# A new order for the attention tile of a decoder kernel, with row-tiled scores and column-tiled value weighting

## What is computed

```python
def _layer(x, wqkv, qs, ksc, wo, lg, lb, w1, b1, w2, b2):   # twice, 8 heads of 64
    qkv = shift_token(x) @ wqkv
    ...
    q, k = l2norm(q) * qs, l2norm(k) * ksc
    q, k = rotary_xpos(q, k)
    # window w of 128 tokens sees the keys of windows w-1 and w, causal and masked
    sim = einsum('bhwid,bhwjd->bhwij', q * 8, look_around(k))
    o = einsum('bhwij,bhwjd->bhwid', softmax(where(mask, -max, sim)), look_around(v))
    x = x + o @ wo
    ...                                      # then layer norm, gated gelu MLP, residual
```

## Time and profile before

| | us |
|---|---|
| median of 3 runs | 1198.59 (1198.31 to 1202.55) |
| the profiled execution | 1197.12 |
| its span, first to last instruction | 1195.40 |
| attention of layer 0, first score to the first MLP product | 393.2 to 669.8 |
| attention of layer 1, the same | 802.3 to 1075.4 |
| one sequence of four tiles in the loop | 67.6 |

### The profile page before, as it was taken

One profiled execution on the slowest core, in us unless ns is written; L12 is line 12 of the kernel. 1 busy time (PEld: TensorE's weight loads), 2 busy tenths in 40 slices (PEclk: granted clock), 3 DMA queues, 4 the chain that ended last, 5 costly groups with the idle time before them and its releaser, 6 DMA issues.

```text
span 1195.4 us, 18259 instructions
## 1 busy us (share of the span) xinstructions
PE 1069.2 (89%) x5720; PEld 881.1 (74%) x5720; DVE 760.0 (64%) x1887; ACT 543.9 (46%) x1188; POOL 366.6 (31%) x375
## 2 busy tenths in 40 slices
PE   5899799999999798999998699998999899879987
PEld 3677667677677687877877478877878787768776
DVE  7777874566666866677665245677767666645463
ACT  4667423030313555556554234445556565544332
POOL 5212421121215644444432000144445435400021
PEclk9899899999999899999999899999999999999999
DMA  8001020000000000000001000000000000000011
GB/s 308 1 1 53 19 93 0 1 0 0 1 1 19 1 1 19 0 18 0 0 28 54 26 9 9 1 19 1 2 18 0 18 0 22 7 6 9 9 38 36
DMA packets 14330, 25.35 MB, mean 21 GB/s; under 512 B 848, under 2 KB 11208, under 8 KB 13512
## 3 DMA queue, kind: packets, MB, share of 16 engines
q1 hardware_dynamic: 14280, 24.72, 6.1%
HBM read 20.53 MB, written 2.10 MB: 19 GB/s over the span
## 4 chain that ended last, share of the span: by engine, by line
PE 62%; DVE 17%; issue 8%; ACT 6%; DMA 4%; POOL 2%; DVEq 0%; POOLq 0%; SPq 0%; ACTq 0%
PE bank L1455 21%; PE bank L1741 8%; PE bank L1768 7%; PE bank L1786 5%; PE bank L1647 5%; PE bank L1599 4%; DMA shifted<-inner 4%; PE bank L1753 4%; PE bank L1871 3%; DVE conv L602 2%; ACT probs_t L1342 2%; ACT probs L1331 1%; PE bank L1610 1%; DVE scores L914 1%; PE bank L1779 1%
## 5 line engine op out<-in xcount | busy, mean ns | idle before, releaser
L1331 ACT ACTIVATE probs<-scores,row_bias,q_rnorm 128x256 f32<-128x256 f32 (+1 forms) x256 | 144.5, 566 | 160.5 <-DVE row_bias L919 159.7
L1768 PEld LDWEIGHTS bank<-v_tok,probs_t 128*128 128x128 f32 x896 | 113.4, 191 | 48.8 <-ACT probs_t L1342 28.1
L1768 PE MATMUL bank<-v_tok,probs_t 128*128 128x64 f32 x896 | 119.4, 273 | 32.4 <-ACT probs_t L1342 18.6
L1741 PE MATMUL bank<-k_t,q_heads 128*128 128x256 f32 (+1 forms) x512 | 118.1, 365 | 9.6 <-DVE q_heads L903 8.1
L914 DVE CUSTOM_DVE_ANT_0 scores<-bank,mask 128x256 f32<-128x256 f32 (+1 forms) x256 | 89.3, 385 | 26.2 <-PE bank L1741 22.7
L1741 PEld LDWEIGHTS bank<-k_t,q_heads 128*128 128x128 f32 x512 | 87.4, 195 | 18.8 <-issue 9.3
L476 POOL TENSOR_TENSOR norms<-norms,minus_half 128x16 f32<-128x16 f32 x32 | 93.6, 2926 | 2.7
L1455 PE MATMUL bank<-wqkv_hi,x_hi 128*128 128x512 f32 x192 | 87.4, 455 | 2.2 <-DVE rot L882 1.4
L1753 PE MATMUL bank<-ident,probs 128*128 128x128 f32 x448 | 72.1, 278 | 6.2 <-ACT probs L1331 6.2
L1455 PE MATMUL bank<-wqkv_lo,x_hi 128*128 128x512 f32 x192 | 76.8, 400 | 0.0
L1455 PE MATMUL bank<-wqkv_hi,x_lo 128*128 128x512 f32 x192 | 76.5, 398 | 0.0
(11 more groups left out here) (234 smaller groups left out, 2710.8 us busy)
## 6 DMA issues: line engine op xcount, KB each, us to landing
w_stage<-in_wm_l_dram SPq DMA_DIRECT2D x8, 534.0 KB, 3.6
w_stage<-in_wqkv_dram SPq DMA_DIRECT2D x2, 1536.0 KB, 7.6
out_dram<-stream SPq DMA_DIRECT2D x4, 512.0 KB, 2.9
shifted<-inner SPq DMA_DIRECT2D x8, 254.0 KB
stream<-in_x_dram SPq DMA_DIRECT2D x1, 1536.0 KB, 12.4
emb<-in_ctx_dram SPq DMA_DIRECT2D x1, 1536.0 KB, 6.6
inner<-in_w_gate_dram SPq DMA_DIRECT2D x1, 1152.0 KB, 8.5
ew<-in_pos_bias_dram SPq DMA_DIRECT2D x1, 1024.0 KB, 9.9
```

The costliest lines, as they stand in the source:

```text
L1331: act.activation(probs[:, i % 2, e, 0:nk], scores[:, i % 2, e, 0:nk], ACT.Exp, bias=row_bias[:, w % 2, h:h + 1], scale=q_rnorm[:, w, h:h + 1],
L1741: ins = pe.matmul(bank[6 + i % 2][:, e * 2 * P:e * 2 * P + nk], q_heads[:, 2 * i + e, :], k_t[:, i, k0:(w + 1) * P], start=True, stop=True)
L1768: ins = pe.matmul(bank[3][:, h * DH:(h + 1) * DH], probs_t[:, i % 2, 2 * e + k, :], v_tok[:, w - nk + 1 + k, h * DH:(h + 1) * DH], start=( ...
```

## The change

One turn is now called `window`. Per tile:

- The queries are copied to `q_t` in one piece by ACT (`queries`); `q_heads`, `q_even` and `q_odd` go, and so does clearing `q_heads`.
- `score_pairs` runs four heads at once (g = 0, 1): each matmul uses 64 rows of the array, e = 0 the upper and e = 1 the lower half, and writes to bank 6 or 7 by e.
- `weigh_values` runs two pairs at once: v is now the stationary operand (64 columns), the transposed probabilities the moving one (128 columns), and the two heads use the two column halves of the array. The result comes out transposed, features on the partitions, in bank 3.
- The inverse row sums are spread by POOL to 128 x 512 (`spread_sums`), transposed by PE (`transpose_sums`) and copied out by ACT (`sums_transposed`); DVE multiplies them onto bank 3 straight into `o_t` (`normalise`). `o_tok`, `transpose_o` and `o_transposed` go.
- The second value group, the sums, the projection and the residual of tile n fall in the turn of tile n+1, for every w. All four scores of tile n are in its own turn.
- The loop is shifted by one tile. In the last tiles the MLP's statistics come one turn earlier, and the MLP's first product no longer waits for the last residual: its banks are 4 and 5, and `c_res` is waited for ahead of the second.

```diff
-            def score(n, w, i):
+            def score_pairs(n, w, g):
+                if g == 0:
+                    pe.wait_ge(c_qt, n + 1)
+                if not (isinstance(n, int) and n == 0 and g == 0):
+                    pe.wait_ge(c_tt, 8 * n + 4 * g)
...
+                for i in (2 * g, 2 * g + 1):
+                    for e in range(2):
+                        half = slice(e * DH, (e + 1) * DH)
+                        ins = pe.matmul(bank[6 + e][:, (i % 2) * 2 * P:(i % 2) * 2 * P + nk], q_t[half, i, :],
+                                        k_t[half, i, k0:(w + 1) * P], start=True, stop=True)
...
+            def weigh_values(n, w, g):
+                pe.wait_ge(c_pt_out, 4 * n + 2 * g + 2)
+                if g == 0:
                     pe.wait_ge(c_v, n + 1)
-                    pe.wait_ge(c_on, n)
+                    pe.wait_ge(c_ot_out, n)
...
+                for i in (2 * g, 2 * g + 1):
                     for k in range(nk):
-                        ins = pe.matmul(bank[3][:, h * DH:(h + 1) * DH], probs_t[:, i % 2, 2 * e + k, :],
-                                        v_tok[:, w - nk + 1 + k, h * DH:(h + 1) * DH], start=(k == 0),
-                                        stop=(k == nk - 1))
+                        for e in range(2):
+                            h = 2 * i + e
+                            ins = pe.matmul(bank[3][e * DH:(e + 1) * DH, i * P:(i + 1) * P],
+                                            v_tok[:, w - nk + 1 + k, h * DH:(h + 1) * DH],
+                                            probs_t[:, i % 2, 2 * e + k, :], start=(k == 0), stop=(k == nk - 1))
...
+            def transpose_sums(n, last=False):
+                pe.wait_ge(c_rb, n + 1)
...
+                    ins = pe.transpose(bank[2][:, i * P:(i + 1) * P],
+                                       rsum_heads[:, 2 * i:2 * i + 2, :].rearrange("p e d -> p (e d)"), ident[:, :])
...
+            def window(n, w, l, prev, one, two, three):
+                score_pairs(n, w, 0)
+                if prev: transpose_sums(n - 1)
+                if two: qkv(n + 2, (w + 2) % TT, 0)
+                if prev: weigh_values(n - 1, (w - 1) % TT, 1)
+                score_pairs(n, w, 1)
+                if two: qkv(n + 2, (w + 2) % TT, 1)
+                transpose_probs(n, w, 0)
+                transpose_probs(n, w, 1)
+                if prev: project_o(n - 1)
+                weigh_values(n, w, 0)
+                if one: transpose_k(n + 1, (w + 1) % 2, [(c_res, n)] if prev else [])
...
+                if two: qkv(n + 2, (w + 2) % TT, 2)
+                if one: transpose_q(n + 1, (w + 1) % 2)
+                transpose_probs(n, w, 2)
+                if three: transpose_x(n + 3, (w + 3) % 2, bank[1][:, 0:D], [(c_rope, 6 * (n + 2) + 6)])
+                transpose_probs(n, w, 3)
...
                 for j in range(KH):
+                    if j == 1:
+                        pe.wait_ge(c_res, NT * (l + 1))
                     mlp_up(m, j)
...
-                pe.wait_ge(c_res, NT * (l + 1))
+                pe.wait_ge(c_pt_out, 4 * NT * (l + 1))
```

More of the change, by code:

```diff
@@ L499, in last_columns, with window @@
                         .then_inc(w1_last, 1)
[L501 to L510, removed]
+            def window(n, t, w, l, b, two, three):
+                if three:
+                    copy_tile(n + 3, t + 3, (w + 3) % 2, l * NB + b + 1 if w == 0 else l * NB + b + 2)
+                if two:
+                    rotate(n + 2, w % 2)
+                elif w == 2:
+                    mlp_rstd(l * NB)
+                spread_sums(n)
+                if two:
+                    rnorm(n + 2, (w + 2) % TT)
+                if w:
+                    split_mlp_weights(l, b, w - 1)
             def mlp_rstd(m):
@@ L941, in att_residual @@
                 dve.tensor_tensor(inner[:, tile, :], inner[:, tile, :], bank[2][:, 0:D], ALU.add).then_inc(c_res, 1)
[L943 to L984, removed]
@@ new lines, in window @@
+            def window(n, t, w, l, prev, one, two, three):
+                masked(n, w, 0)
+                masked(n, w, 1)
+                if two:
+                    rope_products(n + 2, (w + 2) % TT, 0)
+                elif w == 2:
+                    mlp_aggr(l * NB)
+                if prev:
+                    normalise(n - 1)
+                if one:
+                    norm_keys(n + 1, (w + 1) % 2)
+                masked(n, w, 2)
+                masked(n, w, 3)
+                if prev:
+                    att_residual(n - 1, t - 1)
+                if two:
+                    rope_products(n + 2, (w + 2) % TT, 1)
+                invert_sums(n, w)
+                if two:
+                    sum_squares(n + 2)
+                if three:
+                    x_low(n + 3, (w + 3) % TT, bank[1][:, 0:D])
+                elif w == 1:
+                    for i in range(TT):
+                        mlp_stats(l * NB, 0, i)
+                elif w == 2:
+                    mlp_norm(l * NB, 0)
+                else:
+                    input_low(l * NB)
@@ L1326, in exps @@
                 act.wait_ge(c_nb, u + 1)
-                if w or i >= 2:
+                if not (isinstance(n, int) and n == 0 and i < 2):
                     act.wait_ge(c_pt, u - 1)
@@ L1338, in probs_transposed @@
                 act.wait_ge(c_pt, u + 1)
-                if w or i >= 2:
-                    act.wait_ge(c_pv, u - 1)
+                if not (isinstance(n, int) and n == 0 and i < 2):
+                    act.wait_ge(c_pv, 2 * n + i // 2)
                 if w:
@@ L1378, in mlp_input, with sums_transposed @@
-            def mlp_input(m, l):
+            def sums_transposed(n):
+                act.wait_ge(c_rt, n + 1)
+                act.wait_ge(c_ot_out, n)
+                act.activation(rsum_t[:, :], bank[2][:, :], ACT.Copy).then_inc(c_rt_out, 1)
+            def window(n, w, l, prev, one, two, three):
+                if prev:
+                    sums_transposed(n - 1)
+                if two:
+                    square(n + 2, 0)
+                exps(n, w, 0)
+                exps(n, w, 1)
+                if two:
+                    square(n + 2, 1)
+                probs_transposed(n, w, 0)
+                probs_transposed(n, w, 1)
+                exps(n, w, 2)
+                if one:
+                    keys(n + 1, (w + 1) % TT)
+                else:
+                    mlp_scaled(l * NB, l)
+                exps(n, w, 3)
+                if one:
+                    queries(n + 1)
+                if three:
+                    x_transposed(n + 3, (w + 3) % TT, bank[1][:, 0:D])
+                probs_transposed(n, w, 2)
+                if two:
+                    values(n + 2, (w + 2) % TT)
+                probs_transposed(n, w, 3)
+                if not one:
+                    mlp_rounded(l * NB)
```

234 lines of the change are left out of this document (93 added, 141 removed).

## The result

The changed kernel takes 1088.77 us (1083.93 to 1089.57, 4 runs) against 1198.55: ratio 0.907, interval 0.904 to 0.910, so 110 us less. The forecast was 1099. The profiled execution's span is 1082.2 for 1195.4, 113.2 less, and 112.8 of it lies in the two attention stages: from a layer's first score to its MLP's first product 276.5 became 221.2 and 273.2 became 215.8. The MLP of layer 0 takes 132.5 in both, the stretch from the second MLP's first product to the end 119.9 and 120.5; before the first score it is 1.0 less.

The account below looks back on a forecast made before the run. PE was taken to bound the kernel, by its own work, then its waits. Six passes saving 65 us and two layer ends saving 34 took 99 off 1197.1, giving 1098, as median 1099; range for 8 in 10: 1065 to 1148.

Parts of the forecast that it names:

- PE's own work is the first term, its waits the second: Attention loop, pass of four tiles: PE works 60.0 us and waits 7.6 of 67.64.
- Scores, 4.5 saved: Score matmuls with row halves side by side: a wide group takes 5 steps for 8, a pass 7.6 us for 12.1.
- Values, 5.0 saved: Value weighting with column halves side by side: a wide group takes 9 steps for 16, a pass 6.8 us for 11.8.
- Form changes, 4.2 a pass: PE switching between full, row-tiled and column-tiled form: 28 changes at 0.15 us add 4.2 a pass (0 to 8.4).
- Waits, 2.0 a pass: PE waits still left in the loop: 2.0 us a pass (0 to 4), 0.5 a tile.
- The hand layout: Hand-made schedule of a wide turn without form changes: each wait has 0.5 to 1.7 us in hand; PE sets the pace.
- The sums: Row sums' new path: POOL copy 1.26 us; busy DVE 41.7, ACT 40.4, POOL 35.5 a pass, none reaching PE.
- The rival of late sums: Sums come 1.8 us late against 0.8 in hand; PE and ACT stand 1.0 a tile: 1131 us, chance 0.08.
- Last sequence and way into the MLP, 17 each: Each layer's last sequence and way into the MLP: 55.7 us for 72.6, 17 saved, twice 34.
- Rival without concurrency, 1159: Tiled matmuls don't run side by side in either form: 1159 us; no or half concurrency together has chance 0.18.
- Slow rival: Weight loads exposed in tiled form and nothing side by side: a pass 76.9 us, in all 1273, chance 0.04.

Follow-up runs that it names:

- e5: Changed kernel with both heads' scores computed from the upper 64 rows alone; 1127.86 us, ratio 0.940.
- e9: Changed kernel with every value matmul in the left column half, in the order of e6; 1125.77 us, ratio 0.939.
- e1: Changed kernel with each score group running all upper-half matmuls, then all lower-half ones; 1085.88 us, ratio 0.907.
- before: The kernel without the change; 1198.55 us.
- e7: Changed kernel with POOL's spread of the inverse row sums done four times in a row; 1131.27 us, ratio 0.943.
- after: The changed kernel itself; 1088.77 us, ratio 0.907.
- e8: Changed kernel; in each layer's last attention tile, MLP input scaling moved behind the last exps and its normalisation behind the four masked scores; 1077.48 us, ratio 0.8985.
- e10: Changed kernel with scores in the upper row half alone and values in the left column half alone; 1171.46 us, ratio 0.977.
- e11: Kernel before the change with row-tiled scores alone, each pair waiting until the previous pair is masked; 1224.45 us, ratio 1.022.
- e2: Changed kernel with value weighting running all left column-half matmuls, then all right ones; 1106.15 us, ratio 0.923.
- e3: Changed kernel with the loops over heads turned outward in both scores and values; 1106.45 us, ratio 0.922.
- e6: Changed kernel with value weighting in blocks of four matmul instructions per column half instead of two; 1088.43 us, ratio 0.907.

## Why the prediction came out as it did

The direction, the place and the mechanism were right; the gain was 110 for 99 by the medians and 113 by the profiled executions, for which the sum was made. That it is as near as this is in part luck: the loop gave more than I counted and the ends less. Point by point:

- *PE's own work is the first term, its waits the second.* Right: e5 and e9 lengthen a pass by what their steps say, 5.9 for 6.0 and 6.0 for 6.5.
- *Scores, 4.5 saved.* The size was right (7.7 a pass for my 7.6), the step behind it wrong. I let a matmul start only after the one before it, which gave five steps. Each half runs its own row of four steps, 0.86, and 0.20 more go into entering and leaving. The two counts agree by chance; e1 told them apart.
- *Values, 5.0 saved.* 4.5: eight steps of 0.109 and 0.15, 1.02 for my 0.96. That a loaded 64-column operand would go no faster by itself is shown by e9 (1.89 for 1.68).
- *Form changes, 4.2 a pass.* Mis-sized: about 2.0. Only the way back into the full form shows as a loss behind the group, 0.15 to 0.19, three times a tile; the way in is the group's own 0.2 (0.15 at the values), part of which I had counted as a step. Put on one side, eight score groups, eight value groups and the ways back make 1.6 + 1.2 + 2.0 = 4.8 a pass, so the changes together cost about what I gave them; the step too many in each group was what hid it. The Trainium skill (TensorEngine Tiling (Array Packing), Key Properties) says that a change of mode drains TensorE; the pauses of 0.17 and 0.33 in the loads agree with it.
- *Waits, 2.0 a pass.* Mis-sized: 0.2 (53.32 less 53.15). The hand layout with its margins of 0.5 to 1.7 held, and I had added to it out of caution. With the 2.2 of the form changes that is 4.0, less 0.5 at the values and 0.1 at the scores: the 3.4 by which the pass missed (53.3 for 56.7), over six passes 20. Another 2 come from before: its six passes took 67.3 to 69.0, the two longest with 3.4 us at the lower clock.
- *The sums.* POOL's copy took 0.61, half my 1.26; POOL came to 33.3 for 35.5, DVE to 39.6 for 41.7, ACT to 40.2 for 40.4. None reached PE. The rival of late sums needs more than its 0.8: e7 shows its price, 42 us for 2.2 us of delay, and that the narrow turn, with 0.74 in hand, would pay first.
- *Last sequence and way into the MLP, 17 each.* Too high. The six passes, timed one by one, took 408 before and 320 after, 88 of the 112.8 less in the two stages; so all the rest, the last sequences and the first turns, gave 25 for my 34. The DVE's MLP statistics and normalisation ahead of `masked`, which my layout had left out, made the gap that e8 closes.
- *Rival without concurrency, 1159.* e10 puts it at 1171. The pass came out as I had it, 65.1 for 65.2; what I had too high were the ends, 26 for latency. By e10's profile its two stages are 25.7 shorter than before's, of which the six passes have 17.6, so the ends gave 8.
- *Slow rival.* Its mechanism, exposed loads in tiled form, doesn't occur: in one half alone (e5) the score step stays 0.216.

What stays open: the part of e8's gain beyond the 5.1 of its gaps. Executions of one kernel lie up to 6 us apart here, 1083.93 at a mean granted clock of 0.975 and 1089.57 at 0.967 for the changed kernel, so some of it may be that; no run separates it. Open too: what share of e11's loss is the lower clock, column tiling alone in the old order, and whether the old value step of 0.105 was set by its load of 128 columns, as the prediction had it.

## What to carry to other kernels

Where f32 matmuls use half the array's rows or columns, put the two halves' matmuls into one long group: here a group of 8 went from 1.92 to 1.06 us and one of 16 from 1.89 to 1.02, at 0.15 to 0.19 us for each way back to the full form. Short groups with a wait between them, and the lower clock that went with them, lost it again (e11 is 2% slower than before). Read each engine's margin in the shortest turn of the loop, not in the usual one (here 0.74 for 1.15); and before adding caution to a layout by hand, ask which wait it stands for.

## What the runs showed of the hardware

- The array's halves take their matmuls as two rows of their own, and PE passes over waiting matmuls of one half to start the other's: past three in the scores of e1 (0.013 us apart), while in e2 the right half, eight behind, started with the fifth of the left, again past three. So it is in all 64 groups of e1 and all 48 wide groups of e2. The Trainium skill (TensorE: Matmul & The Clock Gate, The mechanism) has matmuls strictly in program order in start and end; for starts in two halves these runs show otherwise (482.655 for the ninth, 482.759 for the sixth in e2). The kernel signals a group's end on its last matmul alone. In every group of after, e1, e2, e3 and e6 that one was also the last to start; no run shows that the signal is safe where the halves are loaded unevenly.
- Inside one half a 64-row f32 matmul instruction costs what a full-height one does, 0.216 us for 256 columns, and its load stays hidden.
- Weight loads pause at a change of form, 0.17 us into the tiled scores and 0.33 out of them.
- The granted clock fell to the lower level behind waits of PE at the ends of the attention: from 597.90 in after, once PE had stood 1.97, and from 609.90 in e8, behind 0.76 and 1.35. A group of eight wide score instructions then took 1.96 for 1.14, a projection 3.68 for 1.99. Not every wait is followed by such a fall: behind those of 1.82 and 1.59 in the same tile of after the clock stayed 1.00.
